# Linear attention: VectorE's feature map, the next batch's statistics and its transposes change places in the slot order

## Time and profile before

| | us |
|---|---|
| median of 3 runs | 3903.14 |
| lowest and highest of the runs | 3900.80, 3903.16 |
| the profiled execution | 3900.51 |
| its span, from the first to the last instruction | 3898.8 |

### The profile page before, as it was taken

One profiled execution on the slowest core, in us unless ns is written; L12 is line 12 of the kernel. 1 busy time (PEld: TensorE's weight loads), 2 busy tenths in 40 slices (PEclk: granted clock), 3 DMA queues, 4 the chain that ended last, 5 costly groups with the idle time before them and its releaser, 6 DMA issues. The chain is left out here.

```text
span 3898.8 us, 93481 instructions
## 1 busy us (share of the span) xinstructions
PE 3564.1 (91%) x28930; PEld 2965.2 (76%) x28930; DVE 2823.7 (72%) x8997; ACT 2180.9 (56%) x6677; POOL 392.4 (10%) x574
## 2 busy tenths in 40 slices
PE   6999999899999998259968889998899999999998
PEld 5888888688888887149946666765788888888887
DVE  5666666577777776646658868886987787777786
ACT  5777777677777776235545548886433333333333
POOL 0000000000000000331178002221000000000000
PEclk9999999999999999679989989999999999999999
DMA  2000000110000000532211000001200000000000
GB/s 99 0 0 0 0 0 0 32 40 11 11 11 11 11 11 28 176 116 77 72 53 44 4 20 22 22 22 42 71 12 13 8 11 13 9 16 8 11 11 9
DMA packets 56111, 109.74 MB, mean 28 GB/s; under 512 B 8368, under 2 KB 27184, under 8 KB 55728
## 3 DMA queue, kind: packets, MB, share of 16 engines
q1 hardware_dynamic: 46656, 80.72, 6.6%
q0 software_dynamic: 8464, 26.22, 2.0%
q10 hardware_dynamic: 864, 1.19, 0.1%
HBM read 72.46 MB, written 35.65 MB: 28 GB/s over the span
## 5 line engine op out<-in xcount | busy, mean ns | idle before, releaser
L639 ACT ACTIVATE c_pr<-c_sm,c_nmx 128x256 f32<-128x256 f32 x512 | 254.5, 499 | 153.6 <-DVE c_nmx L485 153.6
L127 PE MATMUL f_ps_out<-f_out_rounded,f_zgT 128*128 128x256 f32 x1024 | 309.7, 302 | 0.0
L128 PE MATMUL f_ps_out<-f_out_rest,f_zgT 128*128 128x256 f32 x1024 | 288.1, 281 | 0.0
L639 ACT ACTIVATE a_pr<-a_sm,a_nmx 128x128 f32<-128x128 f32 (+1 forms) x512 | 227.3, 445 | 106.1 <-DVE a_nmx L485 106.1
L129 PE MATMUL f_ps_out<-f_out_rounded,f_zgT 128*128 128x256 f32 x1024 | 285.9, 279 | 0.0
L485 DVE CUSTOM_DVE_ANT_0 a_sm<-a_ps_s,causal 128x128 f32<-128x128 f32 (+1 forms) x512 | 152.6, 354 | 164.2 <-PE a_ps_s L371 164.2
L2184 DVE TENSOR_TENSOR f_gv<-f_ps_v,f_gm_step 128x512 f32<-128x512 f32 x256 | 175.9, 687 | 124.2 <-PE f_ps_v L129 112.0
L2343 ACT CAST f_zgT<-f_ps_g 128x512 fp32r<-128x512 f32 x256 | 151.4, 591 | 203.7 <-PE f_ps_g L2073 203.7
L485 DVE CUSTOM_DVE_ANT_0 c_sm<-c_ps_s,c_mask 128x256 f32<-128x256 f32 x512 | 186.8, 421 | 92.0 <-PE c_ps_s L371 90.5
L2243 DVE TENSOR_TENSOR f_zgT<-f_ps_g,f_zgT 128x512 fp32r<-128x512 f32 x256 | 176.6, 690 | 76.2 <-ACT f_zgT L2343 72.5
L127 PE MATMUL f_ps_v<-f_val_rounded,f_xs 128*128 128x512 f32 x512 | 213.2, 416 | 8.5 <-DVE f_gv L2184 8.3
(11 more groups left out here) (380 smaller groups left out, 11428.5 us busy)
## 6 DMA issues: line engine op xcount, KB each, us to landing
f_slot_rows<-f_run POOLq DMA_DIRECT2D x1, 9216.0 KB, 35.0
f_rows<-f_slot_rows SPq DMA_DIRECT2D x72, 128.0 KB, 2.0
f_slot_out<-f_y SPq DMA_DIRECT2D x72, 128.0 KB, 1.9
c_ctx_stage<-in_ctxT SPq DMA_DIRECT2D x32, 256.0 KB, 2.8
small<-in_f_w SPq DMA_DIRECT2D x16, 512.0 KB, 3.9
x_sb<-in_x SPq DMA_DIRECT2D x8, 512.0 KB, 7.8
small<-in_c_w SPq DMA_DIRECT2D x8, 512.0 KB, 4.0
c_mask_stage<-in_mask SPq DMA_DIRECT2D x16, 256.0 KB, 3.0
```

The source lines that it names most:

```text
L127: nc.tensor.matmul(out, sh, mh, start=start, stop=False, **kw)
L128: nc.tensor.matmul(out, sh, ml, start=False, stop=False, **kw)
L639: last = nc.scalar.activation(pr[:, r, i, 0:n], sm[:, j, i, 0:n], ACT.Exp, bias=nmx[:, j, i:i + 1], scale=-1.0, accum_out=sums[:, r, i:i + 1])
```

```diff
             def slot(b, s):
-                if s == STEPS - 1 and (not isinstance(b, int) or b + 1 < B):
+                if softmax and s == STEPS - 1 and (not isinstance(b, int) or b + 1 < B):
                     turn_x(b + 1)
...
                     turn_o(at[2])
+                if not softmax and s == STEPS - 1 and (not isinstance(b, int) or b + 1 < B):
+                    turn_x(b + 1)
...
-                    if s == 0 and (not isinstance(b, int) or b + 1 < B):
-                        measure(b + 1)
                     if ended:
                         finish(*ended)
                     for j in range(J):
+                        if now and s % 2 == 0 and j == s // 2:
+                            features(*now)
                         if one:
                             keep_past(one[0], one[1], j)
-                        if now and s % 2 == 0 and j == 0:
-                            features(*now)
                     if one:
                         fill_v(*one)
+                    if s == 0 and (not isinstance(b, int) or b + 1 < B):
+                        measure(b + 1)
...
-                if s == 1 and (not isinstance(b, int) or b + 1 < B):
+                if s == (1 if softmax else 2) and (not isinstance(b, int) or b + 1 < B):
                     if not softmax:
                         invert(b + 1)
                     normalise(b + 1)
...
-                if not softmax and s == 0 and (not isinstance(b, int) or b + 1 < B):
+                if not softmax and s == 1 and (not isinstance(b, int) or b + 1 < B):
                     take_root(b + 1)
```

## The result

The changed kernel takes 3956.32 us (median of four runs, 3953.74 to 3959.19), the kernel before 3901.97 in the runs beside it (3895.98 to 3903.16). The ratio is 1.014, 95% interval 1.0128 to 1.0152: slower by 54 us, where +19.3 was forecast and 3931 was the top of the range. The profiled execution took 3956.41 us, with a span of 3954.7.

The account below looks back on a forecast made before the run. The prediction took the linear attention's length, with TensorE and VectorE waiting in turn, as what can change. Its terms 22.1 + 2.0 + 0 - 0.8 - 4 = +19.3 us gave 3922 us against the median, range 3899 to 3931.

Parts of the forecast that it names:

- T to T: One round between moments when the next batch's l_xn is ready: 20.14 us instead of 18.44, 13 rounds giving +22.1 us.
- The v projection: TensorE, slot 0: its 1.0 us wait for features goes, and with it VectorE's 0.7 us wait in slot 1.
- The root's 3.01 us: ScalarE, slot 1, ahead of Relu: loads, square root and dummy Exp take 3.01 us, exceeding the gap by 1.90.
- The last batch: Last batch: turnings done while the transposes of x wait, against its last 0.16 us: -0.8 us.
- The first batch: First batch: features some 2 us earlier, later root and l_xn take about as much back: 0, with -2 to +2.
- Rival A: The root in slot 1 is hidden, round 18.3 us: about -3 us, 3900, no change; chance 0.10.
- rival C: TensorE's clock falls from 2.4 to 1.2 GHz for a third of the time: +55 us, about 3977; chance 0.05.
- GpSimd's term: Of the 7.8 us that eight batches lose beside GpSimd, half is absorbed: -4 us, between 0 and -7.8.
- the second batch's round: The round before the steady ones, without output projection: 18.6 us against 16.55, +2.0 us.

Follow-up runs that it names:

- filled waits: The changed kernel with idle transposes in TensorE's waits of slot 3: 12 and 14 in both waits, 3938.51 us, or 14 in one, 3921.37 us.
- the one wait filled: The changed kernel with 14 idle transposes on TensorE in its slot 3 wait for l_xn only: 3921.37 us, ratio 1.005 to the kernel before.
- the third group: Changed kernel with 14 idle transposes, with and without root tables, beside unedited copies: before 3899.98 us (reference 3899.74), after 3953.0 us.
- the first group: Changed kernel without root tables, kernel before with features first alone, and changed kernel with the moved chain alone: 3913.36, 3892.01, 3967.46 us; kernel before 3899.3.

## Why the prediction was wrong

The direction and the chain from the root to l_xn were right, and its figures held. What failed is a resource that the sum left constant, TensorE's clock.

**Held.**
- *T to T.* 20.14 us forecast; 20.14 and 20.15 us measured in the quiet rounds of the two kernels whose filled waits hold the clock there. The root pushes Relu to the end of the dummy Exp, VectorE waits 1.75 us for the map (1.8 forecast), TensorE 2.22 for l_xn (about 2), and the scores of slot 3 find VectorE idle for 0.9 us where the clock is full.
- *The v projection* waits no more, and VectorE's slot 1 for 0.2 us at most.
- *The root's 3.01 us*, two loads of 1.28 us among them, are the same at the new place. The Trainium skill (ScalarE: Activation LUTs, Rules for kernel authors) has some 2.7 us for a switch; no row of before or after shows that.
- *The last batch*, -0.8 forecast: with the one wait filled, 24.71 us pass from the last copy of the turned x to the last z copy, before 25.62, so -0.9. In the changed kernel it is luck that its block's end looks right (32.8 us to the last instruction, before 33.4): 25.71 us pass to the last z copy, nothing gained, and the closing output projection happens to take 3.25 us instead of 3.78.
- *The first batch*, 0 forecast: the second batch's copy is at 1999.39, before at 1999.55. In the third group the unchanged copies of the two kernels have it at 1999.87 and 1998.34, 1.5 us apart, so this shows no more than that nothing large moved.
- *Rival A's price*, 18.3 us for a hidden root: 18.30 measured, by taking the tables away with the clock held.

**Failed: "No row here speaks for it" in rival C.** The prediction saw both waits and named the lower level of the clock, but gave that 0.05 and kept every pitch of TensorE from the earlier trace rows at full speed. The trace of the kernel before has rows in this very block that do speak for it, and others against:

```profile
1988.71 3.78 PE L1443 MATMUL l_ps_p<-small,l_xnT 128*128 128x256 f32 x8 [4.17 <-DVE l_qk L1603]
...
2083.59 1.99 PE L1443 MATMUL l_ps_p<-small,l_xnT 128*128 128x256 f32 x8 [2.04 <-DVE l_qk L1603]
...
2292.46 3.78 PE L1529 MATMUL l_ps_t<-small,l_oT 128*128 128x256 f32 x8 [0.68 <-ACT l_oT L1829]
```

Behind a wait of 4.17 us in the first batch, and behind three short ones at the end of the last (0.49, 0.89 and 0.68 us), eight matmuls take 3.78 us instead of 1.99, at a granted clock of 0.50. Beside GpSimd five single waits of 1.66 to 2.04 us pass at a clock of 1.00. So the rows left open what two waits within 4.8 us would do; 0.05 and a range without it were too little.

Priced by the runs: 14 rounds, 54.2 us more with the clock as granted, and 25.6 us in the kernel with the one wait filled (a round of 19.89 us, then seven of 148.94 together, then six of 20.14). The filling gives back 28.6 us, some 2.0 a round (27.5 against the unchanged copy of its own group); the two whole kernels differ by 32. With the 3.2 us that the filled kernel still loses, the clock costs 31 to 35 us, more than the order. Rival C's own sum, a third of the time on 11 us of the round, gave 3.7 a round; the clock is down for some 3.5 to 6 us of 22.

**GpSimd's term**, -4 with 0 to -7.8 as its ends, comes out nearer to 0, by how much is open. The seven rounds beside GpSimd lost 7.8 us against quiet ones before (136.88 against 7 x 18.44). With the wait filled they lose 8.0 (148.94 against 7 x 20.14), but 3.2 of this is the clock: 4.8 is left, so that 3.0 were absorbed. The unchanged copy of the kernel before in that group lost only 6.9 (135.93 against 7 x 18.43), 1.7 of it by the clock, and against its 5.2 no more than 0.4 was absorbed. In the changed kernel the loss is 7.4 (163.69 against 7 x 22.32), with the clock down in every round. "It hurts only where VectorE is on the path" was right, and GpSimd's work does fall there. The timeline of the changed kernel at l_xn, with the earlier trace rows at 0.29 and 0.74 us for the first two:

```profile
2087.00 1.40 DVE L1614 COPY l_vp<-l_v_all 128x64 f32<-128x64 f32 x2
2088.51 1.33 DVE L1592 TENSOR_SCALAR l_xn<-x_sb,mean_var,l_rstd 128x256 f32 x2
2089.98 1.11 PE L1428 MATMUL l_ps_p<-ident,l_xn 128*128 128x128 f32 x4 [3.93 <-DVE l_xn L1592]
```

These two are now the last steps before `turn_x`. They take 1.70 us longer than in the earlier trace rows, and the wait is 3.93 us instead of the quiet rounds' 2.22, 1.71 longer.

**Mis-sized: the second batch's round**, +2.0 forecast, +3.3 in the kernel with the wait filled, where its wait for l_xn is 1.88 us against 0.61 in the quiet rounds. GpSimd is at work beside this round too, and the sum had no term for that. In the changed kernel it is +4.1.

With 3.3 for this round, -3.0 for GpSimd and -0.9 for the last batch the prediction's sum is 22.1 + 3.3 - 3.0 - 0.9 = 21.5 us, and 24.7 with the 3.2 for the clock. The kernel with the filled wait measured 25.6 in its profiled rounds, 24.7 with its last batch, and 21.6 over all runs. The 28 to 32 us that the filling gives back come on top and make the 54.

**Left open.** Which wait brings the clock down is known for this kernel only by example: 1.71 and 0.61 us with the filling between them do not, 1.71 and 2.22 do in every round, 0.49 and 1.6 do in some rounds and not in others. With the filling between them 1.54 and 2.29 us do and 1.71 and 2.35 do not, and single waits of 2.03 and 2.04 us in the kernel before did once and did not once. So the length of the waits alone does not decide it; what else does was not tried.

## What to carry to other kernels

A step that is moved off one engine's slot lands on another engine's slack: take that slack from the row at the new place (1.40 us here) before the step (3.01 us) is moved there. Price every new wait of TensorE twice, by its length and by what the matmuls behind it cost if the clock is down after it; look in the whole block of before, its beginning and end too, for a group of matmuls that takes twice as long as its like behind a wait. Where there is one, the lower clock belongs in the range. And try the steps of a bundle one at a time: here the first, `features` ahead of one mask, is worth 0.17% by itself and is faster than both kernels, while the moved chain by itself costs 68 us.

## What was not expected of the hardware

- TensorE is busy for 108.94 of 131 us from 2184 to 2315 us, and still it is at the lower clock in every round by the end of its waits of 1.71 and 2.22 us, and back at full speed some 3.5 to 6 us later.
- Matmuls that nobody needs make a kernel faster: 14 transposes, 1.69 us of a wait, give back some 2 us a round, though not every fall of the clock is averted.
- In one group of runs ScalarE waited up to 6.4 us for a releaser outside the trace, in the stretch in which GpSimd fetches rows, and the unchanged kernel took 3919.73 us there instead of 3899, on the same chip as in the first group.
